# V and K of a linear-attention layer turned on VectorE with a pass through DRAM, in place of TensorE's transposes

## The reference

```python
qkv = silu(einsum('bnf,of->bno', x, w_qkv)).reshape(b, n, h, 3 * d)
q, k, v = split(qkv, 3)
def step(kv, blk):                     # blocks of 64 tokens
    qi, ki, vi = blk
    o_inter = einsum('bhmd,bhde->bhme', qi * q_decay, kv)
    qk = einsum('bhmd,bhnd->bhmn', qi, ki) * diag_decay
    o_intra = einsum('bhmn,bhne->bhme', qk, vi)
    return block_decay * kv + einsum('bhmd,bhme->bhde', ki * k_decay, vi), o_inter + o_intra
out = norm_w * out * rsqrt(mean(out * out) + eps)
return einsum('bno,fo->bnf', sigmoid(einsum('bnf,of->bno', x, w_gate)) * out, w_out)
# around it: xn = layernorm(x); result = x + attn(xn) * silu(router_ffn(xn))
```

## Time and profile before

| | |
|---|---|
| median of 3 runs | 1118.34 us (1117.85 to 1118.74) |
| profiled execution | 1118.39 us, span 1116.6 us |
| TensorE busy | 1093.6 us, 98% |
| VectorE, ScalarE, GpSimd busy | 545.1, 630.0, 651.9 us |
| transfers | 83.2 MB, 22.4% of 16 engines |
| TensorE's granted clock, mean | 0.996 |

### The profile page before, as it was taken

One profiled execution on the slowest core, in us unless ns is written; L12 is line 12 of the kernel. 1 busy time (PEld: TensorE's weight loads), 2 busy tenths in 40 slices (PEclk: granted clock), 3 DMA queues, 4 the chain that ended last, 5 costly groups with the idle time before them and its releaser, 6 DMA issues.

```text
span 1116.6 us, 15381 instructions
## 1 busy us (share of the span) xinstructions
PE 1093.6 (98%) x5988; PEld 934.2 (84%) x5988; DVE 545.1 (49%) x965; ACT 630.0 (56%) x1118; POOL 651.9 (58%) x636
## 2 busy tenths in 40 slices
PE   6999999999999999999999999999999999999997
PEld 6788887888888888888888888888888888888886
DVE  6335445454554666554444544534454454434437
ACT  6666466564655646565554655646565554655543
POOL 5865556565655747556475875737456465655613
PEclk8999999999999999999999999999999999999999
DMA  3211111131222323322632421101031131111123
GB/s 133 72 38 57 38 39 38 38 113 58 87 65 76 95 80 104 91 90 71 243 116 83 162 76 56 40 20 57 20 113 58 38 114 38 41 36 46 50 75 114
DMA packets 42473, 83.20 MB, mean 75 GB/s; under 512 B 3488, under 2 KB 17952, under 8 KB 42400
## 3 DMA queue, kind: packets, MB, share of 16 engines
q1 hardware_dynamic: 42400, 82.21, 22.4%
HBM read 66.47 MB, written 15.73 MB: 74 GB/s over the span
## 4 chain that ended last, share of the span: by engine, by line
PE 93%; ACT 2%; DVE 2%; issue 1%; POOL 1%; DMA 0%; SPq 0%; DVEq 0%
PE BS L163 8%; PE BS L165 8%; PE BS L164 8%; PE BA L163 5%; PE BA L165 5%; PE BA L164 5%; PE BD L163 5%; PE PO L694 5%; PE BD L165 5%; PE BD L164 5%; PE PS L625 5%; PE PX L163 5%; PE PX L165 5%; PE PX L164 5%; PE PT L659 4%; PE PO L679 4%
## 5 line engine op out<-in xcount | busy, mean ns | idle before, releaser
L473 POOL TENSOR_TENSOR WL<-ST,WH 128x768 fp32r<-128x768 f32 (+1 forms) x128 | 165.9, 1301 | 165.3 <-ACT WH L469 165.0
L473 POOL TENSOR_TENSOR WL<-STG,WH 128x512 fp32r<-128x512 f32 (+1 forms) x128 | 131.7, 1029 | 163.1 <-ACT WH L469 163.0
L163 PE MATMUL BS<-XH,WH 128*128 128x512 f32 x384 | 162.9, 424 | 0.6 <-ACT VT L542 0.4
L165 PE MATMUL BS<-XH,WL 128*128 128x512 f32 x384 | 151.2, 394 | 0.0
L164 PE MATMUL BS<-XL,WH 128*128 128x512 f32 x384 | 150.0, 391 | 0.0
L759 DVE TENSOR_TENSOR Y<-Y,PX 128x512 f32<-128x512 f32 x104 | 71.3, 686 | 137.1 <-PE PX L165 136.5
L738 DVE TENSOR_TENSOR GL<-G,GH 128x512 fp32r<-128x512 f32 x64 | 72.3, 1130 | 103.0 <-ACT GH L734 103.0
L717 POOL TENSOR_TENSOR SS<-SS,SQ 128x512 f32<-128x512 f32 x60 | 94.1, 1568 | 35.7 <-ACT SQ L709 35.7
L163 PE MATMUL BA<-XH,WH 128*128 128x512 f32 x256 | 107.9, 422 | 0.7 <-ACT BS L534 0.7
L163 PE MATMUL BD<-XH,WH 128*128 128x512 f32 x256 | 104.8, 409 | 1.1 <-DVE Q L549 1.1
L534 ACT ACTIVATE BS<-BA 128x512 f32<-128x512 f32 x64 | 37.3, 582 | 119.2 <-PE BA L165 119.2
(11 more groups left out here) (300 smaller groups left out, 2445.8 us busy)
## 6 DMA issues: line engine op xcount, KB each, us to landing
STG<-in_wp SPq DMA_DIRECT2D x80, 512.0 KB, 3.6
XR<-in_x SPq DMA_DIRECT2D x38, 256.0 KB, 4.0
dgd<-XR SPq DMA_DIRECT2D x16, 256.0 KB, 4.2
dxh<-WT SPq DMA_DIRECT2D x8, 448.0 KB, 3.3
dxl<-XR SPq DMA_DIRECT2D x8, 448.0 KB, 4.5
XH<-dxh SPq DMA_DIRECT2D x7, 512.0 KB, 4.8
XL<-dxl SPq DMA_DIRECT2D x7, 512.0 KB, 5.7
XR<-dgd SPq DMA_DIRECT2D x10, 256.0 KB, 3.9
```

The source lines that it names most:

```text
L163: eng.matmul(o, ah, bh, start=first, stop=False, skip_group_check=skip)
L165: return eng.matmul(o, al, bh, start=False, stop=last, skip_group_check=skip)
L473: a = op("pool", lambda e, dst=dst, src=src: e.tensor_tensor(WL[:, u, dst], src, f32(WH[:, u, dst]), ALU.subtract))
```

## The change

V and K are no longer transposed by TensorE. VectorE transposes squares of 32x32 within each quarter of the partitions, taking every fourth token so that the rows of the result are in order after a regrouping; the tile is written to DRAM as it lies, and read back with the four quarters side by side; ScalarE then copies it into V or, with the decay, into KD. V goes by a new tile VB, the only one of its kind; K goes by the tile P of its sequence (in the last cycle by parts of DQ). Each of the two old functions becomes three: `v_turn`, `v_back`, `v_copy` and `k_turn`, `k_back`, `k_scale`, planned in their own slots, with the copy three or four slots behind the turn. The decay product of `scores` now also waits for `k_scale`.

The blocks of K and Q are exchanged: K is now o = 0 and Q is o = 1, with the weights laid out to match. Scores of b = 1 go from offset 10 to 12 of a head.

```diff
         def q_at(c, r, b):
-            return STG[:, 2, b * T:(b + 1) * T] if c == CYC - 1 and r else Q[:, b, :]
+            return ST[:, b * T:(b + 1) * T] if c == CYC - 1 and r else Q[:, b, :]
...
-            return (k_at if o else q_at)(g // 4, int(k == GQ1), b)
+            return (q_at if o else k_at)(g // 4, int(k == GQ1), b)
...
         def v_turn(c, r, b):
-            wait("pe", tk["vt", c, r, b], tk["ident"], *tk.get("pt", ()))
-
-            def pe(e):
-                for t in range(4):
-                    m = e.transpose(PT[:, chunk(t)], VT[:, r, b, chunk(t)], ident[:, :])
-                return m
-            d = op("pe", pe)
+            wait("dve", tk["vt", c, r, b], tk.get("vb_free"))
+            d = op("dve", lambda e: e.transpose(VB[:, :].rearrange("p (b k j) -> p b k j", b=4, k=4),
+                                                VT[:, r, b, :].rearrange("p (k i b) -> p b k i", k=4, b=4)))
             tk["vt_read", r, b] = d
-            wait("act", d, tk.get(("v_read", b)), *tk.pop(("v_first", b), ()))
-            a = op("act", lambda e: e.activation(V[:, b, :, :], PT[:, :].rearrange("p (t n) -> p t n", t=4), ACT.Copy))
-            tk["v", c, r, b] = a
-            tk["pt"] = (a,)
+            wait("sp", d, tk.get(("v_back", r, b)))
+            tk["v_out", r, b] = dma(s_vw[b], lambda e: e.dma_start(
+                dvt[r, b, :].rearrange("(p n) -> p n", p=128), VB[:, :]))
+
+        def v_back(c, r, b):
+            wait("sp", tk["v_out", r, b])
+            tk["v_back", r, b] = dma(s_vr[b], lambda e: e.dma_start(
+                VB[:, :].rearrange("t (a n) -> t a n", a=4), dvt[r, b, :].rearrange("(a t n) -> t a n", a=4, t=128)))
+
+        def v_copy(c, r, b):
+            wait("act", tk["v_back", r, b], tk.get(("v_read", b)), *tk.pop(("v_first", b), ()))
+            tk["vb_free"] = tk["v", c, r, b] = op("act", lambda e: e.activation(
+                V[:, b, :, :].rearrange("t k (a j) -> t k a j", a=4),
+                VB[:, :].rearrange("t (a k j) -> t k a j", a=4, k=4), ACT.Copy))
...
-            wait("dve", d, tk["dq", h], tk.get(("p_read", b)))
+            wait("dve", d, tk["dq", h], tk.get(("p_read", b)), tk["kd", b])
...
+        def k_place(c, b):
+            if c == CYC - 1:
+                return DQ[:, 2 * b:2 * b + 2, :].rearrange("p a n -> p (a n)")[:, 0:3 * C]
+            return P[:, b, 0:3 * C]
+
         def k_turn(c, r, b):
-            wait("pe", tk["k", c, r, b], tk["ident"], *tk.get("pt", ()))
...
-                for i in range(3):
-                    m = e.transpose(PT[:, chunk(i)], kk[:, chunk(i)], ident[:, :])
...
+            kk, to = k_at(c, r, b), k_place(c, b)
+            wait("dve", tk["k", c, r, b], tk.get(("p_read", b)), tk.get(("kd", b)))
+            d = op("dve", lambda e: e.transpose(to.rearrange("p (b k j) -> p b k j", b=4, k=3),
+                                                kk[:, 0:3 * C].rearrange("p (k i b) -> p b k i", k=3, b=4)))
...
+            wait("sp", d, tk.get(("k_back", b)))
+            tk["k_out", b] = dma(s_kw[b], lambda e: e.dma_start(
+                dkt[b, :].rearrange("(p n) -> p n", p=128), to))
+
+        def k_back(c, r, b):
+            wait("sp", tk["k_out", b])
+            tk["k_back", b] = dma(s_kr[b], lambda e: e.dma_start(
+                k_place(c, b).rearrange("t (a n) -> t a n", a=4),
+                dkt[b, :].rearrange("(a t n) -> t a n", a=4, t=128)))
+
+        def k_scale(c, r, b):
+            h = 2 * (c % NPAIR) + r
+            wait("act", tk["k_back", b], tk["ke"], tk["state"])
+            tk["kd", b] = op("act", lambda e: e.activation(
+                KD[:, :].rearrange("t (k a j) -> t k a j", k=3, a=4),
+                k_place(c, b).rearrange("t (a k j) -> t k a j", a=4, k=3), ACT.Copy, scale=KE[:, h:h + 1]))
...
-            wait("pe", tk["kd"], tk["v", c, r, b])
+            wait("pe", tk["kd", b], tk["v", c, r, b], *tk["pt"])
...
+        def v_steps(c, base):
+            o = int(c < CYC - 1)
+            for s, r, b in ((4, 0, 0), (9, 0, 1), (16 + o, 1, 0), (21 + o, 1, 1)):
+                plan(base + s, v_turn, c, r, b)
+                plan(base + s + 1, v_back, c, r, b)
+                plan(base + s + 4, v_copy, c, r, b)
+
         def heads_of(c, base):
-            steps = (k_turn, scores, states, inter, intra, gate, gate_high, gate_low)
+            steps = (k_turn, k_back, k_scale, scores, states, inter, intra, gate, gate_high, gate_low)
             for r, s in ((0, base + 7), (1, base + 21)):
-                for b, o in ((0, (7, 7, 9, 11, 13, 13, 14, 15)), (1, (11, 10, 13, 15, 17, 17, 18, 19))):
+                for b, o in ((0, (3, 4, 7, 7, 9, 11, 13, 13, 14, 15)), (1, (8, 9, 12, 12, 13, 15, 17, 17, 18, 19))):
...
-            for s, r, b in ((9, 0, 0), (11, 0, 1), (21, 1, 0), (25, 1, 1)):
-                plan(base + s, v_turn, c, r, b)
+            v_steps(c, base)
```

More of the change, by code:

```diff
@@ L51, in build @@
         dxl = nc.dram_tensor("dxl", (128, 14, T), F32, kind="Internal").ap()
+        dvt = nc.dram_tensor("dvt", (2, 2, 128 * T), F32, kind="Internal").ap()
+        dkt = nc.dram_tensor("dkt", (2, 128 * 3 * C), F32, kind="Internal").ap()
         dgd = nc.dram_tensor("dgd", (NB, T, H), F32, kind="Internal").ap()
@@ L68, in build @@
         P = sb("P", [128, 2, T])
+        VB = sb("VB", [128, T])
         KD = sb("KD", [128, 3 * C])
@@ L131, in build @@
         s_stg = [dsem(f"s_stg{i}") for i in range(3)]
+        s_vw = [dsem(f"s_vw{i}") for i in range(2)]
+        s_vr = [dsem(f"s_vr{i}") for i in range(2)]
+        s_kw = [dsem(f"s_kw{i}") for i in range(2)]
+        s_kr = [dsem(f"s_kr{i}") for i in range(2)]
         s_sm = dsem("s_sm")
@@ L560, in q_at @@
         def q_at(c, r, b):
-            return STG[:, 2, b * T:(b + 1) * T] if c == CYC - 1 and r else Q[:, b, :]
+            return ST[:, b * T:(b + 1) * T] if c == CYC - 1 and r else Q[:, b, :]
         def k_at(c, r, b):
-            return ST[:, b * T:(b + 1) * T] if c == CYC - 1 and r else K[:, b, :]
+            return STG[:, 2, b * T:(b + 1) * T] if c == CYC - 1 and r else K[:, b, :]
         def place(g, o, b):
@@ L582, in place_free @@
                 return (tk["st_h"], tk["st_l"]) if o else stg_free[2]
-            return tk.get(("k_read" if o else "q_read", b), ())
+            return tk.get(("q_read" if o else "k_read", b), ())
         def evict(g, o, b, bank, tok):
@@ L1040, in last_heads @@
         def last_heads(c, base):
[L1042 to L1048, removed]
+            v_steps(c, base)
+            for s, f, r, b in ((10, k_turn, 0, 0), (11, k_back, 0, 0), (14, k_scale, 0, 0), (14, scores, 0, 0),
+                               (15, states, 0, 0), (17, inter, 0, 0), (19, intra, 0, 0), (19, save, 0, 0),
+                               (16, k_turn, 0, 1), (17, k_back, 0, 1), (19, k_scale, 0, 1), (19, scores, 0, 1),
+                               (20, states, 0, 1), (21, inter, 0, 1), (23, intra, 0, 1), (23, save, 0, 1),
+                               (18, k_turn, 1, 0), (19, k_back, 1, 0), (21, k_scale, 1, 0), (21, scores, 1, 0),
+                               (23, states, 1, 0), (25, inter, 1, 0),
+                               (22, k_turn, 1, 1), (23, k_back, 1, 1), (25, k_scale, 1, 1), (25, scores, 1, 1),
+                               (24, gate, 0, 0), (25, gate_high, 0, 0),
                                (26, intra, 1, 0), (26, gate_low, 0, 0), (26, gate, 1, 0), (26, states, 1, 1),
@@ L1186, in build @@
             (tk["xb0", 0],), (tk["xb0", 1],), (tk["xb0", 2],), (tk["xb0", 3],), (tk["xm0", 2],))
+        tk["state"] = tk["d1", 3]
         for b in range(2):
@@ L1209, in build @@
         tail_load(5, lambda: stg_free[1], STG[:, 1, 0:T], STG[:, 1, T:2 * T])
-        tail_load(6, lambda: (*tk["k_read", 0], *tk["k_read", 1]), ST[:, 0:T], ST[:, T:2 * T])
-        tail_load(7, lambda: (*tk["q_read", 0], tk["p_read", 0]), STG[:, 2, 0:T], P[:, 0, :])
+        tail_load(6, lambda: (*tk["k_read", 0], *tk["k_read", 1]), STG[:, 2, 0:T], STG[:, 2, T:2 * T])
+        tail_load(7, lambda: (*tk["q_read", 0], tk["p_read", 0]), ST[:, 0:T], P[:, 0, :])
         banks = (PX, BS[0], BA, PS, BS[1], BD, PO, PX)
```

13 lines of the change are left out of this document (3 added, 10 removed).

## The result

The changed kernel takes 1126.18 us (median of 4 runs, 1125.69 to 1128.39) against 1118.54 for the one before on the same chip: a ratio of 1.0072 (95% interval 1.0055 to 1.009). It is slower by 8 us, where 1074 was forecast. The profiled execution has a span of 1126.6 us.

The account below looks back on a forecast made before the run. TensorE was taken as the bound, making 93% of the chain. Removed turns, new waits for K's copy and x's block loads gave 1118.4 - 49.3 + 4 + 1 = 1074 us; eight in ten were held from 1066 to 1104.

Parts of the forecast that it names:

- The price of the turns: On TensorE, 64 turns of V at 0.44 us and 64 of K at 0.33 removed: 49.3 us saved.
- the legs at the median: DRAM trips: V's legs 2.0 us out and 2.6 back, K's 1.9 and 2.4.
- its busy time down by 45 to 70 us by the profile's count and still above 97% of the span: Sign that the forecast is right: TensorE's busy time falls by 45 to 70 us, yet stays above 97% of the span.
- I charge nothing: SP's queue: 256 more waits ahead of weight loads, which have 4 to 9 slots before GpSimd wants them; 0 us.
- 1 us for the cycle of x's blocks: Cycle loading x's second-half blocks: a few trips stand behind those loads; 1 us, bounds 0 and 10.
- the turn starts at about 762.2 and is back by 769, even with a weight load of 512 KB in front: K's trip for head 1, batch 1: back before ScalarE reaches its copy at about 772.8.
- So V must be back by about 779.4 - 0.6 - 0.6 - 0.6 = 777.5, and there is 1.6 us to spare.: V's trip for head 0, batch 0: back at 775.9, in time for ScalarE's copies ahead of TensorE's seventh product.
- the first rival: V's trip returns late, ScalarE waits in slot 8 with L558 behind: 1103 to 1152 us; chance of slower 0.12.
- It is even, late by nothing to about 1 us a cycle. I take 0.25 x 16 = 4 us, with bounds 0 and 16.: VectorE's decay product waits for K's copy, delaying the state updates TensorE needs: 4 us, bounds 0 and 16.
- VectorE's order has no urgent step right behind a turn: VectorE: slow transposes at twice the price make it late by perhaps 0.6 us a cycle, 10 us.
- The second rival: VectorE transposes are slow, reading every fourth word 16 B apart: 10 us more, 1084 us; chance 0.08.
- The clock, left out: TensorE's granted clock: 1.00 (2.4 GHz) through the middle, no long idling expected from the change, so no term.

Follow-up runs that it names:

- e10_v_later: The kernel before with only V's turns moved to VectorE and the DRAM trip, and V's copy for head 0, batch 0 one slot later: 1096.94 us, ratio 0.9808.
- e1_no_trip: The changed kernel with both legs through DRAM left out; ScalarE copies straight from VB and P, so values differ: 1097.45 us, ratio 0.9821.
- e13_half_blocks: The changed kernel with only seven of the 14 loads of x's blocks in cycle 7, the low halves left out: 1117.39 us, ratio 0.9997.
- e7_bulk_apart: The changed kernel with the 14 loads of x's blocks in cycle 7 issued from ScalarE's queue instead of SP's: 1126.88 us, ratio 1.0076.
- e9_own_place: The changed kernel with K's trip in its own tile instead of P; heads 14 and 15 use head 13's decays: 1115.43 us, ratio 0.9977.
- e5_plain_read: The changed kernel without the trips through DRAM, each VectorE transpose reading word after word instead of every fourth word: 1095.48 us, ratio 0.9799.
- both corrections: The changed kernel with K's trip in its own tile (heads 14 and 15 using head 13's decays) and V's copy one slot later: 1110.07 us, ratio 0.9928.

## Why the prediction was wrong

**The price of the turns: right.** Cycle 10 gives back 3.1 us, 4 x 0.77. V alone, once its copy was moved, gave 21 of the 28 us, and TensorE's busy time fell by 27.2 us there (e10_v_later, 1066.5).

**The exchange, the legs at the median, ScalarE's copies: right.** Nothing; 2.0 and 2.8, 1.9 and 2.6 us; 628 and 609 ns.

**The sum: the waits were mis-sized, 5 us against 57.** 1069 is what is left when the turns go; 28.4 us are on top without any trip (e1_no_trip), 28.7 more with the trips. Of the 57, 39 are idle time of TensorE (62 us against 23), and some 8 the slower clock (below). The rest stands in busy time and was not parted: a record of a matmul is 0.39 us long and the next starts 0.22 later, so that a wait shorter than the difference need not show as idle time. The sign "its busy time down by 45 to 70 us by the profile's count and still above 97% of the span" failed: 28.9 us and 94.5%. Four steps of the forecast failed.

*"I charge nothing" for SP's order, and 1 us for the cycle of x's blocks.* I took a lone transfer's time for all trips and looked at the queue's order, not at how full the DMA engines are in each stretch. In cycle 7 a leg takes 8 us, because 7 MB go through there; the medians hide it. It cost 10.3 us in cycle 7, where the bound was 10. That it is the bytes is shown (e13_half_blocks), that it isn't the place in the queue alone too (e7_bulk_apart). In cycles 4, 6, 13 and 14 it is the trip of which I wrote "the turn starts at about 762.2 and is back by 769, even with a weight load of 512 KB in front": 6.8 us. In cycle 13 it took 10.9, with two loads in front, and the trips cost 6.9 us in the four (e1_no_trip); this is a part of the term that I put at nothing. For the 6.7 us of cycle 8, where K's trip stands between the final loads, and for the weight load at the start, that the trips are the cause is shown by e1_no_trip; whether queue or bytes was not tried there.

*"So V must be back by about 779.4 - 0.6 - 0.6 - 0.6 = 777.5, and there is 1.6 us to spare."* The place was the right one and the first rival named it, but with the wrong condition: the legs are at 2.0 and 2.8 us, not 4, and in most cycles V is back in time. The seventh product waits 12.7 us for L565 all the same, 11 times: 4.6 us at the start, where V is late, and 1.1 us each in cycles 0 and 1, where ScalarE works without a pause through six decays (2.5 us, L222) up to L565, and in 2, 3, 11 and 12, where it makes `g_make`'s last step. e1_no_trip waits there as well (8.4 us, 10 times) without any trip: ScalarE has steps there that other cycles have not, and the copy is one more ahead of L565. I worked out one cycle, which has neither decays nor `g_make`, and took it for all 16. One slot later is worth 9 us.

*"It is even, late by nothing to about 1 us a cycle. I take 0.25 x 16 = 4 us, with bounds 0 and 16."* With the wait of L632 for K's copy 10.8 us went (e9_own_place), inside its bounds of 0 to 16, but the mechanism is another one. I followed what queues behind L632 as far as the states on TensorE. In four cycles `g_make` is queued there too; ScalarE waits for it, with V's copy and L565 behind, and the seventh product waits 1.15 us for L565. That is 4.6 us of the 10.8; where the others lie is not shown.

**"VectorE's order has no urgent step right behind a turn".** The second rival was right in its cause: the transposes are 1.5 to 1.6 times as long, through the 16 B step (e5_plain_read), and VectorE is busy for 118 us more, where 80 were forecast. The step of 16 B makes 393 of the 1095 ns. The rule of the Trainium skill that I had set against the change, SBUF — State Buffer, section Door 1: The DMA port swizzle, is a penalty for each access to a new 16-byte line. The traces agree with it, for the two steps that were run. The slow transposes make 2 us of the time, not 10, once the trips are out of the way; with the trips this was not run.

**The clock, left out, since "nothing in the change makes TensorE idle for long".** It was idle for 4 us and more, and behind such a stall the granted clock of a 10 us stretch was 0.83. In the trace of the changed kernel TensorE is busy for 21.6 us at the 1.2 GHz level, before for 5.7. At half the speed that makes some 8 us of the 57 (an estimate, half of the difference), 3.4 of them in cycle 7 and 2.8 in cycle 8, as part of what the trips cost there.

**What stays open.** Cycles 2, 3, 11 and 12 are at 67 us with both corrections and at 65.3 without K's trips. Some 7 us there belong to K's new steps and not to `g_make`'s place alone; which step carries them was not found. It need not be the transfers: without any trip, and without the two corrections, e1_no_trip has the same 68.5 us there as the changed kernel. The later place of scores of b = 1 was not run by itself.

## What to carry to other kernels

Taking work off the bounding engine pays only where every engine that now hands it something is early in every stage: work out the margin in each kind of cycle (first, router, loads, last), not in a quiet one. A copy that waits for a round trip belongs behind the urgent copies of its engine, and a scratch tile that makes one engine wait for another's read should be a tile of its own. Where 7 MB went through in some 40 us, K's write took 3 to 4 times its median, in either queue, and behind two weight loads 2.7 times; look at what is under way in each stage before a trip is put there.

## What the runs showed of the hardware

A 32x32 transpose of fp32 on VectorE took 702 ns for 512 columns and 569 for 384 when it read word after word, and 1095 and 856 ns when it read every fourth word. A 192 KB write took 1.9 us at the median, 5.1 behind two loads of 512 KB, 8.1 with 1 MB of loads just ahead of it amid 7 MB, and 6.5 us when those loads were in another queue; in the leg of 8.1 us the mean share of the DMA engines was 0.85 for 5.0 us and 0.08 for the last 3.1. Behind a stall of TensorE of 4.4 us the granted clock was 0.51 for a stretch, and six matmuls took 1.29 us in place of 0.94.
